# A tokenizer, attention and expert kernel: x turned in pairs of tokens, w1 corrected on VectorE, and new orders of work

## The reference, cut to what matters

```
out = x
for i in 0, 1:  out = tanh(out @ W_in[i] + b_in[i])
out = |core_diag| * out * out
for i in 1, 0:  out = tanh(out @ W_out[i] + b_out[i])
h = convolution of out over time, 15 taps, stride 2        # 8 x 375 x 64
n = layernorm(h)
q, k, v = n Wq', n Wk', n Wv'
h = h + (relu(q k', masked causally) / row_number) v Wo'
n = layernorm(h)
top 2 of 16 experts by n @ gate_w + gate_b, softmax of the two
y = n + sum over the two of weight * (relu(n @ w1[e] + b1[e]) @ w2[e] + b2[e])
out = h + layernorm(y) * gamma + beta
```

## Time and profile before

| | us |
|---|---|
| median of 3 runs | 189.12 |
| lowest, highest | 187.79, 189.24 |
| profiled execution, whole | 186.39 |
| profiled execution, span from first to last instruction | 184.3 |
| TensorE matmul busy in it | 162.3 |
| VectorE busy | 105.5 |
| ScalarE busy | 94.1 |
| POOL busy | 29.7 |

### The profile page before, as it was taken

The page is one execution under the profiler, slowest core; times in us unless marked ns, Lnnn a source line. Parts: engine busy times, 40 slices in busy tenths (PEclk is TensorE's granted clock), DMA queues, the critical chain, the costliest instruction groups (busy, mean ns, idle before and its releaser), DMA issues.

```text
span 184.3 us, 4120 instructions
## 1 busy us (share of the span) xinstructions
PE 162.3 (88%) x1604; PEld 90.4 (49%) x1604; DVE 105.5 (57%) x314; ACT 94.1 (51%) x167; POOL 29.7 (16%) x47
## 2 busy tenths in 40 slices
PE   0897899999587999999989999999999999999800
PEld 0654565665485455533445534545544444555500
DVE  0413557366985778771379965476995356641151
ACT  0342553876435748465464465466565574566310
POOL 7800002000520303200004400020320002200030
PEclk9999999999999999999999999999999999999995
DMA  4566820000000387000689401889010689200001
GB/s 100 110 122 131 195 57 0 4 4 0 0 4 3 100 233 187 2 4 10 169 201 236 105 17 49 209 219 217 4 38 22 182 238 252 49 4 0 4 0 42
DMA packets 15082, 16.22 MB, mean 88 GB/s; under 512 B 8527, under 2 KB 11451, under 8 KB 15062
## 3 DMA queue, kind: packets, MB, share of 16 engines
q1 hardware_dynamic: 14346, 15.31, 33.4%
q10 hardware_dynamic: 589, 0.57, 1.0%
q0 software_dynamic: 128, 0.07, 0.6%
HBM read 14.99 MB, written 0.96 MB: 87 GB/s over the span
## 4 chain that ended last, share of the span: by engine, by line
PE 55%; DMA 14%; issue 11%; DVE 8%; SPq 3%; ACTq 2%; ACT 1%; POOLq 1%; POOL 1%; DVEq 0%
PE y L1010 13%; PE z L996 12%; DMA band<-filt_pad 6%; DMA gate_all<-gates_dram 6%; PE a L928 3%; PE z L894 3%; PE z L974 2%; PE z L867 2%; PE y L894 2%; PE a L937 2%; PE a L829 2%; DMA gates_dram<-gates_t 2%; SPq L353 2%; PE a L914 2%; PE a L958 2%
## 5 line engine op out<-in xcount | busy, mean ns | idle before, releaser
L496 ACT ACTIVATE hid<-z 128x750 f32<-128x750 f32 x64 | 50.6, 796 | 35.5 <-PE z L996 31.9
L1010 PE MATMUL y<-hid,w_s 64*64 64x375 f32 x512 | 58.5, 483 | 0.3 <-ACT hid L496 0.3
L996 PE MATMUL z<-xg,w_s 64*64 64x375 f32 x512 | 58.7, 477 | 0.1
L788 DVE TENSOR_TENSOR xg<-xa_t,gate_all 128x375 f32<-128x375 f32 x60 | 32.5, 552 | 24.2 <-PE z L996 15.1
L996 PEld LDWEIGHTS z<-xg,w_s 64*64 64x64 f32 x512 | 22.3, 132 | 19.7 <-issue 16.8
L1010 PEld LDWEIGHTS y<-hid,w_s 64*64 64x64 f32 x512 | 19.8, 132 | 18.7 <-issue 8.1
L549 POOL TENSOR_TENSOR stat_A<-stat_A,minus_half 125x6 f32<-125x6 f32 x4 | 6.1, 1536 | 68.5 <-DVE stat_A L613 68.5
L549 POOL TENSOR_TENSOR stat_F<-stat_F,minus_half 125x6 f32<-125x6 f32 x4 | 6.2, 1545 | 44.6 <-DVE stat_F L613 44.6
L702 DVE SCALAR_TENSOR_TENSOR attn<-a,causal_cap 125x125 f32<-125x125 f32 (+1 forms) x16 | 5.3, 351 | 11.2 <-PE a L928 10.8
L549 POOL TENSOR_TENSOR stat_T<-stat_T,minus_half 125x6 f32<-125x6 f32 x4 | 5.6, 1390 | 28.8 <-DVE stat_T L613 28.8
L852 PE MATMUL y<-ident,x_in 125*64 125x125 f32 x48 | 4.2, 344 | 4.5 <-POOL minus_half L530 4.5
(11 more groups left out here) (148 smaller groups left out, 215.9 us busy)
## 6 DMA issues: line engine op xcount, KB each, us to landing
gate_all<-gates_dram SPq DMA_DIRECT2D x54, 187.5 KB, 4.1
gate_all<-gates_dram SPq DMA_DIRECT2D x12, 93.8 KB, 2.8
x_in<-in_x_dram SPq DMA_DIRECT2D x4, 187.5 KB
out_dram<-y_out SPq DMA_DIRECT2D x8, 93.8 KB
w_raw<-in_L_ffn_w_dram SPq DMA_DIRECT2D x1, 512.0 KB
w_s<-in_L_ffn_w_dram SPq DMA_DIRECT2D x1, 512.0 KB, 9.8
x_in<-in_x_dram SPq DMA_DIRECT2D x3, 168.0 KB
band<-filt_pad ACTq DMA_DIRECT2D x1, 305.7 KB
```

The source lines that it names most:

```text
L496: act.activation(hid[:, n % HID], z_pair[e % 2][:, :, 0:TO], ACT.Relu).then_inc(hid_ready.sem, 1)
L788: nc.vector.tensor_tensor(xg[:, n % XG], xa_t[g % 2][:], gate_all[:, e], ALU.mult).then_inc(xg_ready.sem, 1)
L996: ins = mm(z[e % 2][b][q, 0:TO], w1_s[f, e, q], xg[f, n % XG], start=True, stop=True)
L1010: ins = mm(y[h][b * D:(b + 1) * D, 0:TO], w2_s[q, e, :], hid[q, (E * g + e) % HID, b], start=e == 0, stop=e == E - 1)
```

## The change

All of it at once:

- **x by token pairs.** Tile c of a turn now holds tokens 6p+2c and 6p+2c+1 of one sequence, so one 125x128 transpose does two tokens: 6 transposes a group instead of 16 matmuls. Partitions hold the two tokens' features (not the two sequences'), columns the sequences. After layer 3, tanh writes the columns of the two sequences interleaved, so stage T.4 still takes columns in tiles of 125.
- **First group's layers in two sets.** For group 0 the columns of each layer are cut into 188 and 187, each by four 64x64 weights, in the banks of y and of the second z pair. T2.0 therefore waits for tanh 3 of group 0.
- **Pair-wide operations.** For groups 1 to 3 one ScalarE operation covers both banks (750 columns) of each tanh, one VectorE operation the bias of T.4. ScalarE now copies the turned x of these groups and makes their squares.
- **Attention on centred tokens.** Sums and variances come from bn_stats and bn_aggr on VectorE, six of each. A.0 turns xc1 = h - mean. The scale of the row enters at A.5: (variance + eps) times the squared row number, to the power -1/2; A.4 uses xv1 = xc1 / (variance + eps). ScalarE's squares for these two LayerNorms go.
- **w1 on VectorE.** w1's first 63 rows are loaded twice (both halves of the partitions), b1 into each 64th, the last row spread over 63 partitions twice by way of DRAM, after x of groups 2 and 3; S.10 to S.13 subtract on VectorE, S.14 likewise for the gates, whose loads go to POOL's queue.
- **F.** VectorE adds the two halves of y, F.1 has half the matmuls; POOL's addition of beta becomes step H on VectorE; the last two operations become six scalar_tensor_tensor, and the last group's second sequence is stored from ScalarE's queue.
- **Order.** W_out is loaded ahead of group 1's x, the biases ahead of the filter; all four lists are new. `keep_warm` has a count of 0 and makes no matmul.

```diff
-            for b in range(PAIR):
-                load_x(sp, 1, b, (0, SPLIT, TOK))
             for b in range(PAIR):
                 sp.dma_start(w_tok[b * D:(b + 1) * D, 2:4, b * D:(b + 1) * D],
                              w_out.rearrange("n d m -> d n m")).then_inc(ld_out, 16)
+            for b in range(PAIR):
+                load_x(sp, 1, b, (0, SPLIT, TOK))
...
-            sp.dma_start(w1_raw[0:D, :].rearrange("h (e f) -> h e f", e=E), w1.rearrange("e h f -> h e f")).then_inc(ld_w1, 16)
...
+            sp.dma_start(last_row[:], w1[:, DX, :]).then_inc(ld_row, 16)
+            for b in range(PAIR):
+                at, last = slice(b * D, b * D + DX), slice(b * D + DX, (b + 1) * D)
+                sp.dma_start(w1_s[at], w1[:, 0:DX, :].rearrange("e h f -> h e f")).then_inc(ld_w1, 16)
+                sp.dma_start(w1_s[last].rearrange("h e f -> h (e f)"), b1.rearrange("e f -> (e f)").unsqueeze(0)).then_inc(ld_w1, 16)
+            sp.wait_ge(w1_blank, 1)
+            sp.wait_ge(ld_row, 16)
+            for b in range(PAIR):
+                sp.dma_start(w1_last[b * D:b * D + DX].rearrange("h e f -> h (e f)"),
+                             last_row[:].rearrange("e f -> (e f)").partition_broadcast(DX)).then_inc(ld_w1, 16)
```

On VectorE (setup and the first LayerNorm):

```diff
+                    es = slice(PIECE * (s - 10), PIECE * (s - 9))
+                    if s == 10:
+                        dve.wait_ge(ld_w1, 16 * 3 * PAIR)
+                    nc.vector.tensor_tensor(w1_s[:, es], w1_s[:, es], w1_last[:, es], ALU.subtract).then_inc(w1_ready, 1)
...
+            def moments(k, g, src):
+                link = chains[k].at(g)
+                for j in range(NJ):
+                    ins = nc.vector.bn_stats(out=halves_of[k][:, j, :], in_=src[:, j, :])
+                link(ins)
+                for j in range(NJ):
+                    ins = nc.vector.bn_aggr(out=mean_var[k][:, j, :], in_=halves_of[k][:, j, :])
+                link(ins)
...
-                    center("T", g, hres[g])
...
+                    moments("T", g, src)
+                    nc.vector.tensor_tensor(xc1[g][:], src, wide(mean_var["T"][:, :, 0]), ALU.subtract)\
+                        .then_inc(ln_cent["T"].sem, 1)
+                    link(nc.vector.tensor_scalar(stat_t[g][:, 1, :], mean_var["T"][:, :, 1], EPS, None, ALU.add))
+                    nc.vector.tensor_tensor(stat_t[g][:, 0, :], stat_t[g][:, 1, :], cnt_sq[:].rearrange("p r b -> p (r b)"),
+                                            ALU.mult).then_inc(ln_var["T"].sem, 1)
+                    nc.vector.reciprocal(stat_t[g][:, 3, :], stat_t[g][:, 1, :]).then_inc(inv_var.sem, 1)
...
-                    nc.vector.tensor_copy(y_t[:, 1], y[1][:, 0:TO]).then_inc(yt_ready.sem, 1)
+                    dve.wait_ge(yt_ready.sem, yt_ready.after(g, 1))
+                    nc.vector.tensor_tensor(y_t[:, 1], y[1][:, 0:TO], y_t[:, 0], ALU.add).then_inc(yt_ready.sem, 1)
```

The beginnings of the lists, as they are now:

```diff
+ tensor T0.0 S0.8 T0.1 T0.2 T1.0 T0.3 T1.1 S0.1 T0.4 S0.2 T1.2 T0.5 T2.0 T1.3 T2.1
+        A0.0 T1.4 A0.1 T3.0 T2.2 A0.2 T1.5 T3.1 A0.3 T2.3 A0.4 T3.2 T2.4 A0.5 T3.3 T3.4 A0.8 T2.5 A1.0 A0.9
+        A1.1 T3.5 A0.12 A1.2 E0.0 E0.1 A1.3 in0.0 E0.2 in0.1 A1.4 in0.2 E0.3 A1.5 out0.0 in0.3 out0.1 in0.4
+ vector T0.0 S0.6 T0.2 S0.8 S0.1 T0.4 S0.5 S0.2 S0.14 T0.6 T0.8 T1.4 A0.2 S0.10 A0.3 S0.11 S0.12 T1.6 S0.13
+        T1.8 A0.5 T2.4 A0.7 T3.4 H0.0 A0.9 A0.10 A0.11 T2.6 E0.0 E0.1 A1.2 E0.2 E0.3 A1.3 T3.6 gate0.4
```

More of the change, by code:

```diff
@@ L23 @@
 XE = 4
+WARM = 0
 ROW = 751
@@ L393, in _ @@
             load_x(act, 0, 1, (0, SPLIT, TOK))
+            for rows, v in ((vec_rows[0:2], b_in), (vec_rows[2:4], b_out), (vec_rows[4:5], core.unsqueeze(0))):
+                n = v.shape[0]
+                act.dma_start(rows, v.unsqueeze(1).broadcast_to([n, PAIR, D])).then_inc(ld_vec, 16)
             act.dma_start(filt_pad[0:1, MID:MID + TAPS], filt.unsqueeze(0)).then_inc(ld_filt, 16)
@@ L533, in _ @@
             nc.gpsimd.memset(xa[:], 1.0).then_inc(const_pool, 1)
+            nc.gpsimd.memset(w1_last[:], 0.0).then_inc(w1_blank, 1)
             pool.wait_ge(const_pool, 1)
@@ L769, in stage_f, with residual @@
                         dve.wait_ge(stored.sem, stored.after(g - 1, PAIR))
-                    nc.vector.tensor_tensor(y_out[:], yn[:], h2_beta[:], ALU.add).then_inc(y_out_ready.sem, 1)
+                    for b in range(PAIR):
+                        for j in range(b, NJ, PAIR):
+                            ins = nc.vector.scalar_tensor_tensor(out=y_out[:, j, :], in0=scaled[:, j, :],
+                                                                 scalar=stat["F"][:, 2, j:j + 1], in1=h2[g][:, j, :],
+                                                                 op0=ALU.mult, op1=ALU.add)
+                        ins.then_inc(y_out_ready.sem, 1)
+            def residual(g, _):
+                if g == 0:
+                    dve.wait_ge(ld_last, 32)
+                dve.wait_ge(ln_cent["A"].sem, ln_cent["A"].after(g, 1))
+                nc.vector.tensor_tensor(h2[g][:], h2[g][:], beta_b[:].broadcast_to([TOK, NJ, D]),
+                                        ALU.add).then_inc(h2_beta_ready.sem, 1)
             def early(g, e):
@@ L797, in _, with keep_warm @@
             pe.wait_ge(const_pool, 1)
+            def keep_warm(_, n):
+                for _ in range(n):
+                    mm(a0[:, 0:P], ident[:], ident[:], start=True, stop=True)
+            keep_warm(0, WARM)
             def setup(_, s):
@@ L876, in stage_t @@
+                    pe.wait_ge(ready.sem, ready.after(g, 2))
+                    for c in range(2):
+                        for r in range(2):
+                            rows = slice(r * D, (r + 1) * D)
+                            ins = mm(banks[r][c * D:(c + 1) * D, 0:HT], w_tok[rows, (0, 1, 3)[s - 1], rows],
+                                     src[g][rows, halves[c]], start=True, stop=True)
+                            if c:
+                                ins.then_inc(said.sem, 1)
                 elif s == 4:
+                    pe.wait_ge(tanh3.sem, tanh3.after(g, 2))
```

403 lines of the change are left out of this document (197 added, 206 removed).

## The result

| | before | after |
|---|---|---|
| median of 20 runs each | 188.32 | 189.75 |
| lowest, highest | 184.83, 190.05 | 187.78, 192.80 |
| profiled execution, whole; span | 186.39; 184.3 | 190.25; 188.5 |
| mean granted TensorE clock in it | 0.988 | 0.947 |

The change made the kernel about 1% slower: the ratio is 1.0126, 95% interval 1.0074 to 1.0178. The ratio compares only the executions within 1.5% of each kernel's fastest; the medians over all twenty lie 0.8% apart. The forecast was 183.8 us, faster.

What follows compares the result with a forecast made beforehand. TensorE was taken as the bound (88% busy), in the head waiting on a chain through VectorE. Experts' stretch -2.6, head -3.0, collisions +1.0, tail -0.7 gave -5.3: span 179.0, median 183.8 us, range 178.5 to 190.

Steps and rivals of the forecast that it cites:

- the allowance: 1.0 us added for the later gates of groups 2 and 3 and other new collisions.
- F.1's records: Experts' stretch, TensorE: 12 records of 1.54 us become 6 of 0.8, saving 0.7 us in each of three groups.
- The LayerNorm's short ops: Head, VectorE: 0.13 us each at 64 wide, 0.10 at 6 wide; twelve take 1.4 us, the stage 2.5.
- rival (b): Short VectorE ops are dear: at 0.29 us each, +7.6 us over four stages, 191.4 us (187 at 0.2); chance 0.10.
- The sign that I named: Sign that the forecast is wrong: TensorE idle over 3 us after E0.0.
- Nothing of this survives: S0.1 ... waits for wo, which landed at 17.39: Head: the time saved before T0.4 is lost, as S0.1 ahead of it waits for wo; T0.4 starts at 17.5.
- I take 33: Head, S0.10 on VectorE: 1.0 MB more at 203 GB/s is 4.9 us, so w1 lands at 33 us.
- each microsecond after 33 is one of the span: Price of w1 landing late at S0.10: one microsecond of span each, since the chain to E0.0 is behind it.
- Rival (c): Head: TensorE stays at half speed in three steps before attention, 4.3 us less 1.4 hidden: 187 us; chance 0.14.
- rival (a): w1 lands late, at 43.8 us, with VectorE waiting at S0.10: 195 us; chance 0.16.
- A3.12 comes six expert steps later ... Cost 0.3, bounds 0 and 2: Gates of groups 2 and 3: A3.12 3.8 us later, so twelve expert steps of 7.6 us cover 7.1; cost 0.3.
- I count 0.5 as gained: Experts' stretch: of 1.8 us that F.1 waited in three times, 0.5 is gained by steps put ahead of it.

Runs made afterwards that it cites:

- e1: Changed kernel with the four w1 subtractions later on VectorE, behind H0.0 and A1.3: 182.72 us, ratio 0.9643 to the kernel before.
- e12: Changed kernel with w1's last row spread for one sequence of each pair only, 504 KB less to load: 185.23 us, ratio 0.9871 to the kernel before.
- e3: Changed kernel with w1's loads and spreads in 64 rows instead of 63 and b1 left out: 188.56 us, ratio 0.9999 to the kernel before.
- e4: Changed kernel with 16 matmuls on constants filling TensorE's wait ahead of A0.4: 186.52 us, ratio 0.982 to the kernel before.
- e2: Changed kernel with a separate y_out for each group, so F2.4 waits for no store: 185.26 us, ratio 0.9798 to the kernel before.
- e8: Kernel before with F alone changed: VectorE adds the halves of y, F.1 has half its matmuls: 187.63 us, ratio 0.9893.
- e5: Changed kernel with the edits of e1 and e2 together: 179.28 us, ratio 0.9474 to the kernel before.
- e10: Changed kernel with w1's last row spread straight from w1, without the row in DRAM: 194.21 us, ratio 1.0271 to the kernel before.
- e6: e5 with A3.9 to A3.11 together on VectorE and A3.12 two expert steps earlier on TensorE: 178.54 us, ratio 0.9515 to the kernel before.
- e9: Changed kernel with w1 loaded ahead of x of groups 2 and 3 on SP's queue: 196.45 us against 188.99 for the kernel before.

## Why the prediction was wrong

| step | forecast | measured |
|---|---|---|
| T0.5 starts | 20.7 | 17.80 |
| A0.0 starts | 25.4 | 22.99 |
| VectorE reaches S0.10 | 31.6 | 28.9 |
| w1 has landed | 33 | 35.3 |
| A0.4 starts | 35.6 | 36.76 |
| A0.8 starts | 46.0 | 49.13 |
| E0.0 starts | 56.7 | 59.12 |
| E0.0 to the last expert | 110.8, with the allowance 111.8 | 119.0 |
| tail | 10.5 | 10.4 |

- **Right.** The place of the loss in the head: S0.10 on VectorE, with the chain to E0.0 behind it. F.1's records, 1.54 to 0.89 us. The LayerNorm's short ops: 0.15 and 0.09 apart, 2.5 us from 20.29 to xv at 22.79, so rival (b) falls. The tail. TensorE's work in the experts' stretch: 112.85 less 3.4 for the two dips is 109.5, forecast 109.9. The sign that I named, over 3 us of idle time after E0.0, came: 6.2 us.
- **Wrong, and hidden in the sum: "Nothing of this survives: S0.1 ... waits for wo, which landed at 17.39".** Nothing waited for wo; S0.1 runs at 14.80. conv_w is copied at 17.13 without a wait for the band. So T0.5 starts 2.9 us before the forecast, and VectorE is at S0.10 2.7 us before it. By luck this changed nothing in the total, since it only made the wait for w1 longer (6.45 us, forecast 1.4); in e1, without that wait, A0.4 starts at 32.89, forecast 35.6. Why wo landed sooner no run shows.
- **Wrong: the landing, "I take 33".** It was 35.3. The size of the term was off, not its kind: e12 shows the queue at 195 GB/s for the last piece, near the 203 of the earlier trace rows that I chose. But my reason for 203, that the pieces of this load are like those of the faster stretch, misread the row: 1669 of its 1912 packets are under 512 B, while w1's own loads go in pieces of 512 B and only the spreads in large ones. The trace after moved 173 and 139 GB/s from 16 to 24 us. 2.3 us, of which 1.2 reached A0.4 (TensorE and VectorE behind it were quicker than forecast).
- **Wrong: what a wait costs, "each microsecond after 33 is one of the span".** A wait of 3.85 us on TensorE took 2.6 us more as clock. Rival (c) had the half clock, but only ahead of attention, and rival (a) the wait, but priced without the clock. From 35.5 to 42.3 us the clock was 0.50, and A0.4 to A0.8 took 12.4 us where e3, at full clock, took 9.8. e4 shows it by itself: E0.0 2.2 us earlier in the trace, 3.2 us of the median. I forecast a gap of about 1 us there and never asked what follows a gap.
- **Wrong: "A3.12 comes six expert steps later ... Cost 0.3, bounds 0 and 2".** The term had nothing for SP. I followed A3.12 on TensorE and VectorE and not there, where it had also changed places with F1.5. That is the 5.49 us wait of F2.4, 2.19 us of TensorE, and the dip after it. e2 prices them at 4.5 us. The rest of the late gates, F2.1's 1.69 us, was in the bounds.
- **Wrong: F.1's waits, "I count 0.5 as gained".** In the changed kernel they grew from 1.8 to 3.5 us over four groups, in e8 by the same 1.7 us. In the experts' stretch it is from 1.0 to 2.2, as 0.8 of the 1.8 that I read lies in the tail. F alone is worth 2.0 us (0.9893, 0.9839 to 0.9947; 0.9 between the medians), where the forecast without these 0.5 gave 2.3.

In sum, against a forecast span of 179.0: +2.4 at E0.0 (2.6 of clock and 1.2 of landing, 1.4 made up elsewhere); +7.2 from there to the last expert (3.4 of two dips, 2.2 behind the store, 2.0 by which the other waits, six of 0.3 to 1.7 us, exceed the 1.9 us of idle time and allowance, less 0.4 of matmuls); -0.1 in the tail. These are the 9.5 us. With both waits out, e5 stands at 179.3, below the 183.8 forecast; the early wo is part of that.

What stays open: what makes the clock fall after E0.0. It did in the traces of the changed kernel, of e1 to e4 and of e10, and not in those of e5, e6, e9 and e12, although the waits right before it (0.44 and 1.07 us) are the same in all. Runs of one kernel differ in it, too: the changed kernel's spans of 186.0 and 191.1 us have clocks of 0.966 and 0.938.

## What to carry to other kernels

A setup step that waits for a late DMA belongs behind the last work that could be done without it on its engine, not where its engine is free: four instructions moved were worth 7 us. When a step changes place, write down what it passes on every queue that issues for it; a store behind twenty loads keeps its buffer. And where TensorE is made to wait in a kernel that kept it busy before, price the gap and also the half clock that can come with it; then look at the granted clock of the stretch behind the gap first.

## What the runs showed of the hardware that was not expected

- Gaps of 2.2 and 3.9 us on TensorE went with 3.4 and 6.8 us at half clock, while the clock stayed at full after the 2.58 us gap of e3 and two gaps of 1.68 and 2.62 us in e12. The wait for the store shows it best: 2.55 us in e1, and half clock behind it; 2.62 us in e12, and none. The length of the gap alone does not tell which it will be.
- In the changed kernel the first of the two one-row loads of b1 (8 KB) kept SP's queue for 5.31 us (6.83 in e12), the second for 1.40, where other issues of the same stretch take 0.3 to 1.2. It need not be the load: in e3, which has no b1, the second load of w1 (512 KB), issued at the same time, kept the queue for 5.46 us. The cause stays open.
